# A decoder layer on one core: gram stage with broadcast decays, and 24 projection products dealt over the joins

## The chip, the cores and the metric

One core of a Trainium2 chip runs the whole program. The metric is the device time of one execution in microseconds, the median of several runs. TensorE multiplies, VectorE (DVE), ScalarE (ACT) and GpSimd (POOL) work elementwise, SyncE (SP) issues the DMAs. The matmul accumulators are eight banks of PSUM; GpSimd doesn't touch them.

## The reference, cut to what matters

The layer has three parts, each on a layernorm of x and added to x: a gated delta-rule attention with 16 heads, a cross attention, and eight experts of which one is chosen. The change touches the first alone. Inputs: 4 sequences of 512 tokens, 512 channels; a head has 128 channels for q, k, v and z.

```
qkv = silu(causal_conv4(x @ Wqkv))              # q, k, v of each head
beta = sigmoid(x @ Wb);  g = -exp(A_log) * softplus(x @ Wa + dt_bias)
q, k = l2norm(q) * DK ** -0.5, l2norm(k)
def step(M, inp):                               # M: 128 x 128 per head and sequence
    M = M * exp(g_t)
    M = M + outer(k_t, (v_t - k_t @ M) * b_t)
    o_t = q_t @ M
out = rmsnorm(o) * norm_w * silu(x @ Wz);  y = out @ Wout
```

The kernel computes the recurrence in chunks of 128 tokens. With Gamma(t) the running product of exp(g) in a chunk, it needs the decays between any two tokens of a chunk, exp(G(t) - G(s)), the decays from the chunk's beginning, exp(G(t)), the matrix of scaled products k_s . k_t under these decays, and the inverse of one plus its strict triangle.

## The kernel before

**Order.** TensorE's instructions are written out for all 16 heads. ScalarE, VectorE, GpSimd and SP have head 0, a loop over heads 1 to 14, and head 15. All queues run in program order; each wait is a semaphore wait written by hand. B = 4 sequences, NC = 4 chunks, so a [128, 512] tile usually holds one chunk of the four sequences, 128 columns each.

**Projections.** A head has 16 jobs (JOBS, line 58): K, V, Q and Z for each of the four sequences. A job is 12 products of 512 columns (4 slices of the 512 channels, each high x high, low x high and high x low of values split in two; `proj`, line 560). Seven jobs of the next head, 84 products, are done ahead (`ahead`, line 674), as a filling between dependent steps of this head: 12 before the last job, JOIN_FILL = 7, 2, 2, 1 in the joins, and FILL (60) in the chunk loop. `job_waits` (line 567) lets a job wait until its bank has been read.

**Gram stage** (the loop at line 615, per chunk c). GpSimd makes gt, the triangle times the gate's high and low parts (`decays`, line 1735). TensorE: two products of after_r with gt into bank 3 (the decays between tokens), four transposes of kT, two products of ones_r with gt (the decays from the chunk's beginning, the same in all partitions), four gram products kT x kT, and in chunks 0 and 1 six products each of the job V3. ScalarE: the exponential of the decays to pT, the squares of k with their sums (k_sq), the exponential to gam. VectorE: k_inv and cvec (reciprocal of the squared norm over beta), k_tok (a copy of the transposes), and nT = gram x pT, after GpSimd has scaled pT by cvec (`scaled`, line 1749). In chunk 3 VectorE does k_sqe and the split of the Z weights before nT.

**Jobs.** Then come Q0, Q1, Z0, Q2, Z1, Q3, Z2, 12 products ahead, Z3, with transposes of v after each Z job and of q between (`v_transpose`, `q_transpose`). The four q transposes share bank 2, and the one of sequence b waits until ScalarE has squared the one of b - 1 (qsq_done). Z0 uses the bank of V3 and waits for its convolution on VectorE.

**The inverse.** SP stores the diagonal 32x32 blocks of nT to DRAM and loads their 16x16 blocks; GpSimd inverts these by substitution (line 1783), SP stores and loads back to t32. From there TensorE joins blocks of 16 to 32, to 64, to 128 (`join16_y` to `join64_z`, lines 707 to 785), each a group of small products, with a copy on ScalarE or VectorE between two groups. GpSimd multiplies kT and qT by gam (kdT, qT), waiting for gam_done.

**Chunk loop** (line 807). The state is carried over the four chunks, with 60 products of the next head in between.

## Time and profile before

| | us |
|---|---|
| median of 3 runs | 2017.62 (2013.75 to 2017.89) |
| the profiled execution | 2019.99 |
| its span | 2018.3 |
| TensorE busy in the span | 1908.4 (95%) |
| VectorE, ScalarE, GpSimd busy | 1128.2, 933.0, 743.3 |
| mean granted clock of TensorE | 0.962 |

Times in rows are in microseconds from the span's start, of one profiled execution. PE is TensorE's matmul, PEld its weight load, DVE VectorE, ACT ScalarE, POOL GpSimd, SPq SyncE's queue. A group of instructions is told by its line and its tiles, out<-in. What stands in brackets behind a row is the idle time before it and what ended it. Busy times of consecutive matmuls overlap, since they are pipelined: their pace is that from start to start. The heads of the attention fill the span from 80 to about 1570 us; before it x is normalised and split, behind it come the output product, the cross attention and the experts.

### The profile page before, as it was taken

How to read it: one execution, taken by the hardware profiler on the slowest of the kernel's cores; microseconds unless marked ns; L12 is line 12 of the kernel's file. 1: busy time of each engine (PE TensorE's matmuls, PEld its weight loads, DVE VectorE, ACT ScalarE, POOL GpSimd, SP SyncE). 2: the span in 40 equal slices, each digit the busy share in tenths (PEclk: the TensorE clock that was granted, in tenths of full speed). 3: DMA queues.
4: the chain of work that ended last, by engine and by line, in shares of the span. 5: the costliest groups of instructions: out<-in, count | busy, mean ns of one | idle time of the engine just before them, and what ended most of it. 6: DMA issues, size and time to landing. Idle time of an engine off the chain costs nothing.

```text
span 2018.3 us, 45513 instructions
## 1 busy us (share of the span) xinstructions
PE 1908.4 (95%) x16962; PEld 1558.9 (77%) x16962; DVE 1128.2 (56%) x2048; ACT 933.0 (46%) x2987; POOL 743.3 (37%) x1143
## 2 busy tenths in 40 slices
PE   6899999999999999999999999999997799999999
PEld 4688888888888888888888788888887565656574
DVE  6656566565657465655657574656564352524333
ACT  2556464646455555646465655546463221213121
POOL 1345363645445353636264544536361000000000
PEclk9899899999989899989999998999897899999999
DMA  3011111201021111112020111111113503121200
GB/s 117 6 33 40 25 37 28 43 22 38 22 42 29 32 40 25 34 25 44 21 43 22 38 30 35 40 24 36 25 30 145 156 21 94 42 84 52 61 23 21
DMA packets 220198, 87.12 MB, mean 43 GB/s; under 512 B 138320, under 2 KB 204240, under 8 KB 219280
## 3 DMA queue, kind: packets, MB, share of 16 engines
q1 hardware_dynamic: 220048, 84.83, 16.6%
q8 instruction: 130, 2.13, 0.4%
q14 instruction: 20, 0.16, 0.0%
HBM read 57.28 MB, written 27.53 MB: 42 GB/s over the span
## 4 chain that ended last, share of the span: by engine, by line
PE 60%; issue 21%; DVE 9%; ACT 5%; POOL 4%; DMA 1%; POOLq 0%; DVEq 0%; SPq 0%; ACTq 0%
PE bank L562 27%; PE bank L871 4%; DVE vT L1383 3%; PE bank L821 3%; PE bank L830 2%; PE bank L783 2%; PE bank L772 2%; PE bank L691 2%; PE bank L815 2%; ACT vv L1084 2%; PE bank L837 1%; PE bank L934 1%; PE bank L952 1%; PE bank L669 1%; PE bank L659 1%
## 5 line engine op out<-in xcount | busy, mean ns | idle before, releaser
L562 PE MATMUL bank<-x_hi,w_hi 128*128 128x512 f32 x1024 | 429.8, 420 | 14.7 <-DVE vT L1383 14.3
L562 PE MATMUL bank<-x_hi,w_lo 128*128 128x512 f32 x1024 | 408.9, 399 | 1.8 <-issue 1.8
L562 PE MATMUL bank<-x_lo,w_hi 128*128 128x512 f32 x1024 | 406.5, 397 | 0.0
L562 PEld LDWEIGHTS bank<-x_hi,w_hi 128*128 128x128 f32 x1024 | 196.0, 191 | 55.6 <-issue 13.4
L562 PEld LDWEIGHTS bank<-x_hi,w_lo 128*128 128x128 f32 x1024 | 195.7, 191 | 45.6 <-issue 2.2
L562 PEld LDWEIGHTS bank<-x_lo,w_hi 128*128 128x128 f32 x1024 | 196.6, 192 | 32.0 <-issue 0.6
L1383 DVE SCALAR_TENSOR_TENSOR qT<-bank,cw,qT 128x511 f32<-128x511 f32 (+2 forms) x192 | 142.1, 747 | 51.0 <-ACT qT L1033 46.5
L1848 POOL TENSOR_TENSOR rstd<-ve,mhalf 128x1 f32<-128x1 f32 x32 | 17.4, 544 | 390.2 <-DVE ve L1607 390.2
L1216 ACT ACTIVATE o_tmp<-bank 128x128 f32<-128x128 f32 x256 | 67.4, 278 | 179.0 <-PE bank L837 179.0
L1383 DVE SCALAR_TENSOR_TENSOR vT<-bank,cw,vT 128x511 f32<-128x511 f32 (+2 forms) x192 | 143.0, 745 | 8.6 <-ACT vT L1033 4.1
L1383 DVE SCALAR_TENSOR_TENSOR kT<-bank,cw,kT 128x511 f32<-128x511 f32 (+2 forms) x192 | 143.4, 747 | 5.0
L1816 POOL TENSOR_TENSOR o_rstd<-o_ms,minus_half 128x4 f32<-128x4 f32 x64 | 70.5, 1101 | 200.4 <-DVE o_ms L1525 200.4
L1805 POOL TENSOR_TENSOR qT<-qT,gam 128x512 f32<-128x512 f32 x48 | 59.9, 1275 | 182.0 <-PE bank L691 182.0
L1821 POOL TENSOR_TENSOR state<-state,gam 128x512 f32<-128x512 f32 x32 | 33.6, 1051 | 209.0 <-PE bank L837 204.7
L871 PE MATMUL bank<-wo_hi,o_hi 128*128 128x512 f32 x256 | 105.4, 412 | 0.0
L871 PE MATMUL bank<-wo_hi,o_lo 128*128 128x512 f32 x256 | 100.0, 391 | 0.0
L871 PE MATMUL bank<-wo_lo,o_hi 128*128 128x512 f32 x256 | 100.0, 391 | 0.0
L1484 DVE STREAM_TRANSPOSE tT<-t 128x512 f32<-128x512 f32 x64 | 39.9, 680 | 98.3 <-DMA t<-blkT_d 98.3
L837 PE MATMUL bank<-w,pT 128*128 128x128 f32 x512 | 92.0, 277 | 0.0
L1210 ACT ACTIVATE w<-bank 128x512 f32<-128x512 f32 x64 | 38.3, 598 | 111.1 <-PE bank L821 111.1
L1118 ACT ACTIVATE nv<-bank,k_norm 128x128 f32<-128x128 f32 x256 | 72.9, 374 | 33.0 <-PE bank L669 33.0
L1788 POOL TENSOR_TENSOR prod<-blkN,blkT 128x15 f32<-128x15 f32 (+7 forms) x240 | 65.9, 275 | 54.2 <-DMA blkN<-blkN_d 36.7
(221 smaller groups left out, 4447.3 us busy)
## 6 DMA issues: line engine op xcount, KB each, us to landing
w_raw<-in_w_heads SPq DMA_DIRECT2D x64, 256.0 KB, 2.8
o_d<-og SPq DMA_DIRECT2D x64, 256.0 KB, 2.6
o_raw<-o_d SPq DMA_DIRECT2D x16, 1024.0 KB, 6.2
x_in<-in_x SPq DMA_DIRECT2D x16, 256.0 KB, 3.6
blkN_d<-nT SPq DMA_DIRECT2D x64, 64.0 KB, 2.0
t<-blkT_d SPq DMA_DIRECT2D x64, 64.0 KB, 2.4
wo_raw<-in_w_out SPq DMA_DIRECT2D x4, 1024.0 KB, 9.5
x_res<-in_x SPq DMA_DIRECT2D x16, 256.0 KB, 2.8
```

What stands on the lines that cost most here:

```text
L562: last = mm(bank[bk][:, :], w[:, kind % 2, d, :], xx[:, d, b * S:(b + 1) * S], start=(n == 0), stop=(n == 3 * ND - 1))
L691: last = mm(grid(5 + 2 * (c % 2))[:, b, :], kT[:, b, c, :], qT[:, b, c, :], start=True, stop=True)
L772: last = mm(large(half_bank(g), LATE, i, b), nT[EARLY, b, c, LATE], t32[EARLY, b, c, EARLY], start=True, stop=True)
L821: last = mm(grid(3)[:, b, :], tT[:, b, c, :], nv[:, b, c, :], start=True, stop=True)
L837: last = mm(grid(4)[:, b, :], pT[:, b, c, :], w1[:, c % 2, b, :], start=(c == 0), stop=True)
L871: last = mm(bank[c % 2][:, :], o[:, c % 2, k, :], w[:, k, :], start=(n == 0), stop=(n == 3 * H - 1))
L1118: last = fn(nv[:, b, c, :], grid(6)[:, c, :], ACT.Copy, scale=k_norm[:, b, c:c + 1])
L1216: last = fn(o_tmp[:, b, :], grid(4)[:, b, :], ACT.Square, accum_out=o_sq[:, c, b:b + 1])
L1383: stt(d[:, k:S], bank[JOB_BANK[JOBS.index((kind, b))]][:, 0:S - k], cw[:, kind, TAPS - 1 - k:TAPS - k], d[:, k:S], ALU.mult, ALU.add).then ...
L1788: tt(products, blkN[:, j, j + 1:BLK].unsqueeze(2).to_broadcast([P, below, j + 1]), blkT[:, j, 0:j + 1].unsqueeze(1).to_broadcast([P, below ...
L1805: tt(qT[:, :, c, :], qT[:, :, c, :], gam[:, :, c, :], ALU.mult).then_inc(qg_done, 1)
L1816: tt(o_rstd[:, c, :], o_ms[:, c, :], minus_half[:, 0:B], ALU.pow).then_inc(orstd_done, 1)
```

## The change

1. The decays from the chunk's beginning are no longer made by products with ones in each chunk. TensorE makes them once, for all heads, in chunk 2 of head 0 (`gam_sums`: four products with the triangle, rows are head, sequence and chunk), ScalarE takes one exponential to gam_rows, SP stores them to DRAM, and per head SP loads three chunks' rows, broadcast to all partitions (`load_gam`), behind the loads of blkN and ahead of the next K weights. gam loses chunk 0. GpSimd waits for gam_in.
2. The transposes of kT use banks 2, 0, 4, 2, and that of chunk 2 waits for nothing. The V3 job is dealt 3 products to each chunk instead of 6 and 6; its tap on ScalarE and the split of the Z weights come behind the loop.
3. VectorE makes nT of chunk c - 1 behind the key scales and k_tok of chunk c. The last nT is made from gram, cvec and pT by four steps of 128 columns, without waiting for GpSimd's scaling, which now waits for it. k_tok of chunk 3, k_sqe and the split of the Z weights come behind it.
4. The 12 products before the last job go to the joins, which now have 24: JOIN_FILL names the step ahead of which they stand.
5. In ScalarE's joins the tap of the next K1 comes behind both keep64_y. Three waits (kg, qg, sg) go from the beginning of ScalarE's head. The four semaphores at the heads' end become one.

The diff, cut to its core:

```diff
@@ -62,7 +62,8 @@
 FILL = ((0, 6), (9, 9), (9, 9), (9, 9))
-JOIN_FILL = (7, 2, 2, 1)
+JOIN_FILL = {"z16": 8, "y32_0": 4, "y32_1": 3, "z32_0": 3, "z32_1": 3, "y64_0": 1, "y64_1": 1, "z64": 1}
+assert sum(JOIN_FILL.values()) + sum(sum(f) for f in FILL) == AHEAD * 3 * ND
 HALVES = 2
...
@@ -143,7 +144,7 @@
     nT = sb("nT", [P, B, NC, P])
-    gam = sb("gam", [P, B, NC, P])
+    gam = sb("gam", [P, B, NC - 1, P])
     gt_0 = sb("gt_0", [P, 2, B, P], F32R)
...
@@ -248,13 +250,9 @@
-    def gam_bank(c):
-
-        return 4 if c else 7
-
     def ktr_bank(c):
-        return (2, 0, 0, 2)[c]
+        return (2, 0, 4, 2)[c]
...
@@ -417,6 +415,22 @@
                 sp.dma_start(o_raw[:, c % 2, :, :], o_d[:, :, b, c, :].rearrange("h p t -> p h t")).then_inc(o_in[c % 2], 16)
+
+            def load_gam(h):
+
+                if isinstance(h, int) and h == 0:
+                    sp.wait_ge(gam_done, 1)
+                    sp.dma_start(gam_d.rearrange("(i h) b c t -> (h b c) i t", i=2), gam_rows[:, :, :]).then_inc(gam_out, 16)
+                    sp.wait_ge(gam_out, 16)
+                else:
+                    sp.wait_ge(sg_done, 2 * h)
+                    hold(sp, "sp")
+                    sp.wait_ge(kg_done, 3 * h)
+                    sp.wait_ge(qg_done, 3 * h)
+                    hold(sp, "sp")
+                sp.dma_start(gam[:, :, :, :].rearrange("p b c t -> p b (c t)"),
+                             gam_d[h][:, 1:NC, :].rearrange("b c t -> b (c t)").unsqueeze(0).to_broadcast([P, B, (NC - 1) * P])
+                             ).then_inc(gam_in, 16)
...
@@ -437,6 +451,7 @@
                     sp.dma_start(blkN[rows, :, :], blkN_d[:, :, sl, sl].rearrange("k u s t -> (k u) s t")).then_inc(blkN_in, 16)
+                load_gam(h)
                 if more:
...
@@ -610,21 +624,31 @@
+            def gam_sums():
+
+                for i in range(2):
+                    for n, part in enumerate((g_hi, g_lo)):
+                        rows = part[:, i * H // 2:(i + 1) * H // 2, :, :].rearrange("p h b c -> p (h b c)").bitcast(F32)
+                        last = mm(bank[6][:, i * P:(i + 1) * P], rows, tri[:, :], start=(n == 0), stop=(n == 1))
+                last.then_inc(gam_mm, 1)
+
             def head(h, first, more):
...
                     pe.wait_ge(decay_done, 4 * h + c)
-                    hi, lo = gt[c % 2][:, 0, :, :], gt[c % 2][:, 1, :, :]
-                    mm(bank[3][:, :], after_r[:, :], hi, start=True, stop=False)
-                    mm(bank[3][:, :], after_r[:, :], lo, start=False, stop=True).then_inc(decay_mm, 1)
+                    mm(bank[3][:, :], after_r[:, :], gt[c % 2][:, 0, :, :], start=True, stop=False)
+                    mm(bank[3][:, :], after_r[:, :], gt[c % 2][:, 1, :, :], start=False, stop=True).then_inc(decay_mm, 1)
                     if c == 0:
...
                         pe.wait_ge(conv_done, 12 * h + conv_index(V_, 2) + 1)
-                    read = (0, 0, 2, 1)[c]
-                    pe.wait_ge(ksq_done, 4 * h + read)
-                    pe.wait_ge(ktok_done, 4 * h + read)
+                    if c == 2 and first:
+                        gam_sums()
+                    if c != 2:
+                        read = (0, 0, 0, 1)[c]
+                        pe.wait_ge(ksq_done, 4 * h + read)
+                        pe.wait_ge(ktok_done, 4 * h + read)
                     for b in range(B):
...
@@ -632,20 +656,13 @@
                             out_transpose(h - 1, NC - 1)
-                    pe.wait_ge(gam_done, 4 * h + c)
-                    mm(bank[gam_bank(c)][:, :], ones_r[:, :], hi, start=True, stop=False)
-                    mm(bank[gam_bank(c)][:, :], ones_r[:, :], lo, start=False, stop=True).then_inc(gam_mm, 1)
-                    if c == 1:
-                        pe.wait_ge(gam_done, 4 * h + 1)
                     pe.wait_ge(nT_done, 4 * h + max(c - 1, 0))
...
                         job_waits(h, 2 * B - 1)
-                        proj(V_, B - 1, JOB_BANK[2 * B - 1], 0, 3 * ND // 2)
-                    if c == 1:
-                        proj(V_, B - 1, JOB_BANK[2 * B - 1], 3 * ND // 2)
+                    proj(V_, B - 1, JOB_BANK[2 * B - 1], 3 * c, 3 * c + 3)
...
@@ -691,12 +710,11 @@
-                pe.wait_ge(ktok_done, 4 * h + 3)
-                pe.wait_ge(ksq_done, 4 * h + 3)
+                pe.wait_ge(ktok_done, 4 * h + 2)
+                pe.wait_ge(ksq_done, 4 * h + 2)
                 for job in range(2 * B, NJ):
                     if job == NJ - 1:
-                        ahead(3 * ND)
                         q_transpose(b - 1)
...
@@ -787,19 +806,23 @@
                 join16_y()
-                ahead(JOIN_FILL[0])
+                ahead(JOIN_FILL["z16"])
                 join16_z()
                 qk(3)
-                ahead(JOIN_FILL[1])
+                ahead(JOIN_FILL["y32_0"])
                 join32_y(0)
-                ahead(JOIN_FILL[2])
+                ahead(JOIN_FILL["y32_1"])
                 join32_y(1)
+                ahead(JOIN_FILL["z32_0"])
                 join32_z(0)
-                ahead(JOIN_FILL[3])
+                ahead(JOIN_FILL["z32_1"])
                 join32_z(1)
+                ahead(JOIN_FILL["y64_0"])
                 join64_y(0)
+                ahead(JOIN_FILL["y64_1"])
                 join64_y(1)
+                ahead(JOIN_FILL["z64"])
                 join64_z(0)
...
@@ -1083,12 +1103,11 @@
                     last.then_inc(ksq_done, 1)
-                    act.wait_ge(gam_mm, 4 * h + c + 1)
-                    fn(gam[:, :, c, :], grid(gam_bank(c)), ACT.Exp).then_inc(gam_done, 1)
-                    if c == 2:
-                        split(h, Z_)
-                    if c == 1:
-                        tap(h, V_, 3)
+                    if c == 1 and first:
+                        act.wait_ge(gam_mm, 1)
+                        fn(gam_rows[:, :, :], bank[6][:, 0:2 * P].rearrange("p (i t) -> p i t", i=2), ACT.Exp).then_inc(gam_done, 1)
+                tap(h, V_, 3)
+                split(h, Z_)
...
@@ -1195,10 +1214,10 @@
                 keep32_n(1)
+                keep64_y(0)
+                keep64_y(1)
                 if more:
                     tap(h + 1, K_, 1)
-                keep64_y(0)
-                keep64_y(1)
...
@@ -1452,13 +1470,36 @@
                     nc.vector.reciprocal(cvec[:, :, c], k_inv[:, :, c]).then_inc(cvec_done, 1)
+
+                def keys_kept(c):
                     copy(k_tok[:, :, c, :], grid(ktr_bank(c))).then_inc(ktok_done, 1)
-                    if c == 3:
-                        ts(k_sqe[:, :, :], k_sq[:, :, :], EPS_L2, None, ALU.add).then_inc(kvec_step, 1)
-                        split(h, Z_)
+
+                def masked_gram(c):
                     dve.wait_ge(gram_mm, 4 * h + c + 1)
                     tt(nT[:, :, c, :], grid(5 + 2 * (c % 2)), pT[:, :, c, :], ALU.mult).then_inc(nT_done, 1)
+
+                def last_masked_gram():
+
+                    c = NC - 1
+                    dve.wait_ge(gram_mm, 4 * h + c + 1)
+                    dve.wait_ge(cvec_done, 4 * h + c + 1)
+                    dve.wait_ge(decay_done, 4 * h + c + 1)
+                    for b in range(B):
+                        last = stt(nT[:, b, c, :], grid(5 + 2 * (c % 2))[:, b, :], cvec[:, b, c:c + 1], pT[:, b, c, :],
+                                   ALU.mult, ALU.mult)
+                    last.then_inc(nT_done, 1)
+
+                for c in range(NC):
+                    key_scales(c)
+                    if c < NC - 1:
+                        keys_kept(c)
+                    if c:
+                        masked_gram(c - 1)
+                last_masked_gram()
+                keys_kept(NC - 1)
+                ts(k_sqe[:, :, :], k_sq[:, :, :], EPS_L2, None, ALU.add).then_inc(kvec_step, 1)
+                split(h, Z_)
...
@@ -1734,7 +1772,7 @@
-                pool.wait_ge(gam_mm, 4 * h + max(c - 1, 0))
+                pool.wait_ge(decay_mm, 4 * h + max(c - 1, 0))
                 if c == 1:
...
@@ -1750,6 +1788,8 @@
                     pool.wait_ge(cvec_done, 4 * h + c + 1)
+                    if c == NC - 1:
+                        pool.wait_ge(nT_done, 4 * h + NC)
                     tt(pT[:, :, c, :], pT[:, :, c, :], spread(cvec[:, :, c]), ALU.mult).then_inc(lc_done, 1)
...
@@ -1796,13 +1836,13 @@
                                             pattern=[[0, B], [1, P]], channel_multiplier=-1).then_inc(masked, 1)
-                pool.wait_ge(gam_done, 4 * h + 4)
+                pool.wait_ge(gam_in, 16 * h + 16)
                 for c in range(1, NC):
-                    tt(kdT[:, :, c - 1, :], kT[:, :, c, :], gam[:, :, c, :], ALU.mult).then_inc(kg_done, 1)
+                    tt(kdT[:, :, c - 1, :], kT[:, :, c, :], gam[:, :, c - 1, :], ALU.mult).then_inc(kg_done, 1)
                 pool.wait_ge(qk_mm, 4 * h + 4)
                 for c in range(1, NC):
-                    tt(qT[:, :, c, :], qT[:, :, c, :], gam[:, :, c, :], ALU.mult).then_inc(qg_done, 1)
+                    tt(qT[:, :, c, :], qT[:, :, c, :], gam[:, :, c - 1, :], ALU.mult).then_inc(qg_done, 1)
```

## Rows read from the trace of the kernel before

**Rows 1.** The page, parts 1 and 2: busy times; granted clock in 40 slices.

```profile
PE 1908.4 (95%) x16962; PEld 1558.9 (77%) x16962; DVE 1128.2 (56%) x2048; ACT 933.0 (46%) x2987; POOL 743.3 (37%) x1143
...
PEclk9899899999989899989999998999897899999999
```

**Rows 2.** Windows of one head each: stretch, us, busy per engine, clock, DMA; sum last.

```profile
80.25:170.25 90.00, 87.66 (x950) 75.95 (x948) 56.64 (x95) 51.20 (x169) 43.06 (x65) 1.00 0.13 28
...
265.47:354.38 88.91, 87.66 (x956) 76.01 (x954) 56.68 (x96) 51.24 (x175) 44.92 (x68) 1.00 0.15 34
...
1099.75:1190.97 91.22, 87.85 (x955) 76.20 (x954) 56.67 (x96) 51.23 (x175) 44.85 (x68) 1.00 0.15 33
...
1378.78:1474.55 95.77, 92.42 (x956) 80.30 (x954) 56.76 (x96) 51.24 (x175) 44.98 (x68) 0.95 0.14 31
sum 1394.30, PE 1356.51 PEld 1176.67 DVE 850.97 ACT 768.48 POOL 671.20; mean PE 90.43 PEld 78.44 DVE 56.73 ACT 51.23 POOL 44.75
```

**Rows 3.** Windows inside joins: two whole joins, two late stretches, and what followed one.

```profile
309.40:323.90 14.50, 14.22 (x508) 12.18 (x509) 10.55 (x19) 8.18 (x21) 4.26 (x4) 1.00 0.01 3
...
1143.70:1160.50 16.80, 14.37 (x508) 12.36 (x509) 9.95 (x18) 8.18 (x21) 4.26 (x4) 1.00 0.02 4
...
319.90:323.90 4.00, 3.98 (x67) 3.85 (x65) 3.67 (x6) 2.25 (x4) 0.52 (x1) 1.00 0.00 0
...
222.00:225.90 3.90, 3.14 (x146) 2.30 (x139) 2.80 (x6) 2.10 (x6) 3.04 (x3) 1.00 0.02 4
225.90:232.50 6.60, 6.07 (x71) 5.91 (x70) 3.76 (x6) 2.25 (x4) 0.52 (x1) 0.64 0.00 0
```

**Rows 4.** Timeline of the gram stage: start, us, engine, line, operation, tiles; idle before.

```profile
266.91 1.28 ACT L1079 ACT_TABLE_LOAD   x1
...
268.21 0.60 ACT L1079 ACTIVATE pT<-bank 128x512 f32<-128x512 f32 x1
...
269.20 0.40 PE L619 MATMUL bank<-gt,after_r 128*128 128x512 f32 x1
...
274.16 1.05 POOL L1753 TENSOR_TENSOR pT<-pT,cvec 128x512 f32<-128x512 f32 x1
...
277.36 1.05 PE L642 MATMUL bank<-kT 128*128 128x128 f32 x8
278.17 0.47 PE L562 MATMUL bank<-x_hi,w_hi 128*128 128x512 f32 x1
```

**Rows 5.** Timeline of the gram stage's end: VectorE, and TensorE's wait.

```profile
279.41 0.73 DVE L1457 TENSOR_SCALAR k_sqe<-k_sq 128x16 f32<-128x16 f32 x1
...
280.66 0.68 DVE L1461 TENSOR_TENSOR nT<-bank,pT 128x512 f32<-128x512 f32 x1
...
281.92 2.30 DVE L1383 SCALAR_TENSOR_TENSOR vT<-bank,cw,vT 128x511 f32<-128x511 f32 x3
...
284.37 0.47 PE L562 MATMUL bank<-x_hi,w_hi 128*128 128x512 f32 x1 [0.47 <-DVE vT L1383]
```

**Rows 6.** Before the last q job: ScalarE's timeline, and the chain's moved products.

```profile
300.14 1.14 ACT L1118 ACTIVATE nv<-bank,k_norm 128x128 f32<-128x128 f32 x4
...
301.90 0.33 ACT L1100 ACTIVATE vv<-bank 128x128 f32<-128x128 f32 x1
...
300.49 2.75 PE bank L562 x12
```

**Rows 7.** Timeline where the joins begin: VectorE's and TensorE's first step.

```profile
307.17 2.49 DVE L1484 STREAM_TRANSPOSE tT<-t 128x512 f32<-128x512 f32 x4 [6.08 <-DMA t<-blkT_d]
...
309.35 1.25 PE L719 MATMUL bank<-t,nT 16*32 16x16 f32 x128 [0.24 <-ACT vv L1100]
```

**Rows 8.** DMA issue of the nearest size (KB, us to landing); kdT's writer and reader.

```profile
o_raw<-o_d SPq DMA_DIRECT2D x16, 1024.0 KB, 6.2
...
302.19 3.79 POOL L1801 TENSOR_TENSOR kdT<-kT,gam 128x512 f32<-128x512 f32 x3
...
328.11 1.16 PE L815 MATMUL bank<-state,kdT 128*128 128x128 f32 x8
```

51 lines of the change are left out of this document (23 added, 28 removed).

## The prediction

> **What bounds the kernel now.** I read the page's busy times first: TensorE is busy 95% of the span, no other engine over 56% [rows 1]. So the span is TensorE's list of work plus its waits, at whatever clock it is granted. The reader is to see next that the clock line of the same page is not all nines. I therefore cut the span into heads, from the first decay product of one head to that of the next, with the granted clock beside each [rows 2]. Fifteen such stretches take 1394.30 us. In five of them the clock was 1.00 throughout: 90.00, 88.91, 89.99, 89.32 and 91.22 us (the first, the second and the last of them are shown), together 449.44, mean 89.89. The other ten, of which the last is shown, had a part at the lower of TensorE's two levels (1.2 instead of 2.4 GHz) and take 1394.30 - 449.44 = 944.86 us, mean 94.49. A clock fall thus costs 4.6 us of a head, and the ten cost 46 us. That is the largest single sum in this profile that is neither work nor dependency.
>
> Where does it fall? The joins of a head (from the first 16x16 product to the first product with the inverse) show it. In the head that begins at 265.47 they take 14.50 us at clock 1.00; in the head before, the stretch 222.00 to 225.90 ends the full clock: there PE was busy 3.14 of 3.90 us, with 32x32 and 64x64 products only, and the stretch behind it runs at 0.64 [rows 3]. The comparable stretch of the good head had PE busy 3.98 of 4.00 us. So the clock falls where TensorE has little and small work, in the second half of the joins, where today five projection products (2, 2 and 1) stand among eight groups of small ones.
>
> **Part 1, the broadcast decays.** Each token chunk drops two products of gt with a matrix of ones. Twelve 512-column products take 2.75 us in the chain, 0.23 us each [rows 6], so eight of them are 1.8 us of TensorE work per head, and ScalarE drops four exponentials (0.6 us each, as the one in [rows 4]). Instead, four 128-column products for the whole kernel, one exponential, one store, and per head one broadcast load of 4 x 384 x 4 bytes to 128 partitions, 768 KB. Its nearest row is a 1024 KB load that lands in 6.2 us [rows 8]; by bytes that is 4.7 us, and since its pieces are others I bound it by 4 and 12 and take 6 us. It is issued behind the blkN loads, and its first reader is the kdT product at 302.19 on GpSimd [rows 8], over ten microseconds later, with the substitution between. The weight loads queued behind it on SP are read later still. Its SP waits are for events of the head before, long past. In head 0 SP waits for the store, once, some 3 us, also covered. Cost nothing; uncovered it would be up to 6 us a head.
>
> Does the removed 1.8 us shorten the gram stage? It was 12.7 us long (265.47 to 278.17) and TensorE hardly waited [rows 2, 4]. I replay it from the rows. After the first chunk's decay, transposes, gram and now three projections, TensorE is free 1 us before ScalarE has finished the table load (266.91, 1.28 us) and the exponential behind it (268.21, 0.60 us), which the next decay product waits for [rows 4]: that product starts at about 268.85 instead of 269.20. At the end GpSimd sets the pace: its fourth decay tile and the scaling of chunk 1 end at 275.2 (274.16 + 1.05 [rows 4]), VectorE then makes nT of chunk 1 (0.68 us, as in [rows 5]), and the gram product of chunk 3 waits for that: it starts at about 276.1. Before it started at 277.36 [rows 4]; the eight products less would put it at 275.6. Three projections instead of none stand behind it (+0.7). I get the end of the stage 0.5 us earlier, and two new waits of 0.3 to 0.9 us in place of the products. Bounds: 0 and -1.8 us per head.
>
> **Part 2, pipelined VectorE steps and the last product in one step.** Today k_sqe (held up to 280.14 while GpSimd works) and the weight split stand before the last nT, which ends at 281.34 [rows 5]. Behind the change the last nT needs the column vector only, not GpSimd's scaling: four 128-column steps instead of one of 512, some 1.0 us, ending near 279.1. That is 2.2 us earlier for the block inverse. But the inverse is not late now: VectorE gets t32 at 307.17, TensorE begins the joins at 309.35 when ScalarE has finished the last q squares [rows 7]. So this is slack, worth nothing by itself. k_tok of chunk 3, k_sqe and the split move behind it, in front of the convolution of V3; that convolution starts at about 281.5 against 281.92, and the Z0 job, which waited 0.47 us for it until 284.37 [rows 5], still waits, and starts 0.5 us earlier. The gain of the gram stage and this wait are the same 0.5 us.
>
> **Part 3, twelve products moved.** Twelve projections (2.75 us [rows 6]) leave the place before the last q job and go into the joins, which then hold 24. What did they cover? The next q transpose uses a bank that ScalarE still reads for the previous q squares: nv from 300.14, then squares to 302.2 [rows 6]. Without the twelve, TensorE stands from 300.5 to 302.4, so 2.0 us come back as a wait and only 0.75 us are gained. In the joins the twelve cost 2.75 us, less the waits they cover. The five full-clock heads have joins of 16.60, 14.50, 15.60, 15.00 and 16.80 us (the second and the last are shown in [rows 3]), mean 15.70, for the same list of work; so 1.2 us on average is wait beyond the clean head. There PE's busy time is 14.22 of 14.50, but the ends of small products are modelled, and each of the eight groups begins behind a copy of ScalarE or VectorE; for these handovers I estimate another 0.7 us. 2.75 - 1.2 - 0.7 = +0.8 us per head; bounds 0 and +2.75.
>
> Sum per head: -0.5 - 0.75 + 0.8 = -0.45, and -7 us over the fifteen heads that have products ahead.
>
> **Part 4, the clock.** After the change four or three products stand before each of the four 32-wide groups and one before three of the four 64-wide ones, 16 where there were 5: no stretch of the joins is left with neither large products nor full pace. I expect seven of the ten falls to go net, one or two of the remaining being new ones in the 2.0 us stand of Part 3, which has only transposes around it. 7 x 4.6 = -32 us. Bounds 0 and -46.
>
> The Trainium skill, "TensorE: Matmul & The Clock Gate", in the part on PE-mode transpose, says that transposes do not count as activity for the clock. No row here decides it. By it new falls would come at the stand of Part 3, between transposes, in as many heads as lose one in the joins; that is rival B below, at its 2011 us, and has its chance there.
>
> **Sum.** The profiled execution took 2019.99 us (span 2018.3). 2020.0 - 7 - 32 = 1981 us. The median of the runs is 2.4 us below the profiled one, so I say 1980.
>
> **Rivals.** (A) The forecast: most falls go, the schedule gains little. 1980, own range 1962 to 2000, chance 0.64.
> (B) The falls stay, at the old place or at the stand before the last q job. For it: heads with the same list of work fall and do not fall, so the granted clock hangs on something finer than the list, and the new stand after the Z2 job gives it another place. Against: the starved stretch gets eleven of the twelve products. Time 2018 - 7 = 2011, with one or two fewer 2004. Chance 0.14.
> (C) All falls go and the gram stage gives its whole 1.8 us, because GpSimd and ScalarE start their chain earlier too: per head -1.8 - 0.75 + 0.3 = -2.25, so 2018 - 34 - 46 = 1938. For it: PE at 95%. Against: the replay. Chance 0.13.
> (D) Slower. The joins are bound by TensorE itself, not by waits, so the twelve cost their full 2.75 us there, while the q bank takes 2.0 of the 2.75 us back: +2.0 us per head, +30, the gram stage gives nothing, and half of the falls stay (-23): 2025. It decides from the point where the joins grow by more than 2 us a head and fewer than six falls go. Chance 0.07.
> (E) The broadcast decays come late, so that the change does not take work off the path but puts a transfer on it: a wait on GpSimd before kdT. It would need a load over 15 us; and still TensorE first reads kdT at 328.11 [rows 8], over 20 us after GpSimd makes it. 2 in 100, with a time near 2015.
>
> **How the numbers follow.** Likeliest is A: 1980. The range that holds 8 in 10 must reach into C and B: 1952 to 2011. A measurement of this kernel can tell about 0.2%, 4 us, from no change. Faster by more: A, C and most of B, 0.87. Within: the rest of B and E, 0.07. Slower: D, 0.06.
>
> **What would show it.** Step 1: in a full-clock head the first q job starts 12.2 us after the head's first decay product instead of 12.7; ScalarE's table load ends the wait before the second decay product. Part 3: an idle time of about 2 us before a q transpose, released by ScalarE's squares. Joins: about 16 us with 24 products. Part 4: of the fifteen heads about twelve at clock 1.00, the clock line of the page nearly all nines. I am wrong if heads at clock 1.00 differ from 89.4 by more than 1.5 us, or if over six heads still show a fall.

## The result, and the profile after

The changed kernel takes 2024.44 us (median of 16 runs, 2018.74 to 2036.68), the kernel before 2017.67 (median of 16 beside it); the ratio is 1.0052, with a 95% interval of 1.0035 to 1.0070. It is slower by half a per cent, where 1980 was forecast, outside the range (1952 to 2011). Its profiled execution took 2036.68 us (span 2034.8), 16.7 more than that of before (2019.99). It is the slowest of the 16, 12.2 us above the median, with a mean granted clock of 0.973, where the median of the 16 is 0.980: what follows shows more lost clock than a usual execution of this kernel has.

The changed kernel's page: busy time and count, granted clock in 40 slices, and the broadcast load. They answer [rows 1] and the nearest load of [rows 8].

```profile
PE 1884.1 (93%) x16842; PEld 1516.1 (75%) x16842; DVE 1157.8 (57%) x2096; ACT 904.0 (44%) x2924; POOL 741.2 (36%) x1141
...
PEclk9999999999999999999799999999997899999999
...
gam<-gam_d SPq DMA_DIRECT2D x16, 768.0 KB, 4.9
```

TensorE is busy for 24.3 us less, fewer digits of the clock line lie under nine, and still the span is longer. So time went into waits. Windows of the changed kernel, one head each, columns as in [rows 2]:

```profile
453.40:545.25 91.85, 87.42 (x947) 74.57 (x946) 58.85 (x99) 49.40 (x171) 44.78 (x68) 1.00 0.17 41
...
914.03:1019.60 105.57, 99.08 (x947) 83.54 (x946) 58.38 (x99) 49.39 (x171) 44.70 (x68) 0.87 0.16 36
...
1111.60:1208.36 96.76, 89.23 (x947) 75.68 (x946) 58.81 (x99) 49.41 (x171) 44.76 (x68) 0.98 0.16 39
...
sum 1414.15, PE 1337.17 PEld 1137.60 DVE 878.98 ACT 741.37 POOL 669.62; mean PE 89.14 PEld 75.84 DVE 58.60 ACT 49.42 POOL 44.64
```

The eight heads at clock 1.00 take 92.09 us in the mean, where those of before took 89.89. Seven heads still show a fall, most of them short, one of 27 us (the second row shown). The fifteen heads are 1414.15 - 1394.30 = 19.9 us longer; the first begins 3.3 us earlier.

What TensorE waited for in heads 1 to 14 of the changed kernel (tile and line, what ended the wait; us in all, times, longest):

```profile
PE bank L676 <- ACT vv L1119: 27.6, 14, 2.0
PE bank L661 <- DVE nT L1480: 12.5, 28, 0.6
PE bank L640 <- ACT pT L1099: 10.3, 14, 0.7
PE bank L576 <- DVE vT L1401: 8.1, 14, 0.6
PE bank L749 <- issue: 5.7, 6, 2.1
...
PE bank L738 <- issue: 2.5, 1, 2.5
PE bank L710 <- issue: 2.0, 1, 2.0
```

The first row is the stand ahead of the last q job, 2.0 us in each of 14 heads. The second and third are the gram stage's new waits, 22.8 us or 1.6 us a head, against 1.8 us of products removed. The fourth is the Z0 job, which waits for VectorE's convolution of V3; the kernel before has this wait too (0.47 us, [rows 5]). The "issue" rows, waits that no semaphore ended, turned out to be the key to the rest.

The gram stage, changed kernel, head at 453.40 (answers [rows 4, 5]): VectorE, GpSimd and TensorE.

```profile
459.32 0.82 DVE L1470 SCALAR_TENSOR_TENSOR k_inv<-k_sq,beta_inv_h 128x4 f32<-128x4 f32 x1 [0.37 <-ACT vv L1104]
...
462.20 0.95 DVE L1470 SCALAR_TENSOR_TENSOR k_inv<-k_sq,beta_inv_h 128x4 f32<-128x4 f32 x1 [0.67 <-ACT vv L1104]
...
465.60 0.17 DVE L1470 SCALAR_TENSOR_TENSOR k_inv<-k_sq,beta_inv_h 128x4 f32<-128x4 f32 x1 [1.06 <-ACT vv L1104]
...
459.06 1.05 POOL L1793 TENSOR_TENSOR pT<-pT,cvec 128x512 f32<-128x512 f32 x1
...
462.08 1.05 POOL L1793 TENSOR_TENSOR pT<-pT,cvec 128x512 f32<-128x512 f32 x1
...
464.60 1.16 PE L661 MATMUL bank<-kT 128*128 128x128 f32 x8 [0.26 <-DVE nT L1480]
465.51 0.48 PE L576 MATMUL bank<-x_hi,w_hi 128*128 128x512 f32 x1
...
466.29 0.40 PE L576 MATMUL bank<-x_hi,w_hi 128*128 128x512 f32 x1
...
472.49 0.47 PE L576 MATMUL bank<-x_hi,w_hi 128*128 128x512 f32 x1 [0.57 <-DVE vT L1401]
```

An operation of four columns takes 0.17 us at 465.60, where GpSimd is idle, and 0.82 and 0.95 us where it starts under a GpSimd operation: it ends at 460.14 and 463.15, within 0.04 us of GpSimd's end (460.11, 463.13). My replay did not lengthen them. These rows alone suggest that VectorE waits for GpSimd here; no run took GpSimd's operation away. The Trainium skill ("GPSIMD Engine Reference", the specification table) has the two engines share their access to SBUF, with contention when a VectorE instruction reads two inputs from it, as this one does; the rows agree.

TensorE's rows give the end of the stage. The last gram product starts 11.2 us into the head (464.60; before 11.9, and the replay had 10.6). Three products of V3 follow (from 465.51), and the first q job starts at 466.29, 12.9 us into the head, where the kernel before starts it at 12.7 and the forecast was 12.2. So the eight products less did not shorten the stage at all.

### The profile page after: what moved, and what is told of

Its sections match the earlier page's. It is cut to its first block, busy times and chain, and to the rows that moved or that the text cites. A ratio compares the mean times of both kernels' runs of the same rounds, so it can differ in the third digit from the quotient of the medians.

```text
span 2034.8 us, 45304 instructions
## 1 busy us (share of the span) xinstructions
PE 1884.1 (93%) x16842; PEld 1516.1 (75%) x16842; DVE 1157.8 (57%) x2096; ACT 904.0 (44%) x2924; POOL 741.2 (36%) x1141
## 4 chain that ended last, share of the span: by engine, by line
PE 67%; issue 15%; ACT 9%; DVE 8%; DMA 1%; POOL 1%; ACTq 0%; DVEq 0%; SPq 0%; POOLq 0%
PE bank L576 31%; PE bank L894 4%; PE bank L844 3%; PE bank L860 3%; ACT vv L1104 3%; PE bank L838 2%; PE bank L853 2%; PE bank L859 2%; PE bank L710 2%; PE bank L791 2%; PE bank L802 2%; DVE vT L1401 2%; ACT vv L1119 2%; ACT nv L1137 2%; PE bank L957 1%
## 5 line engine op out<-in xcount | busy, mean ns | idle before, releaser
L576 PE MATMUL bank<-x_hi,w_hi 128*128 128x512 f32 x1024 | 434.6, 424 | 16.3 <-DVE vT L1401 15.8
L1793 POOL TENSOR_TENSOR pT<-pT,cvec 128x512 f32<-128x512 f32 x64 | 67.2, 1050 | 60.0 <-DVE nT L1489 51.1
L1376 DVE TENSOR_TENSOR w_lo<-w_raw,w_hi 128x512 fp32r<-128x512 f32 x64 | 47.9, 749 | 68.4 <-ACT w_hi L1045 68.4
L661 PE MATMUL bank<-kT 128*128 128x128 f32 x512 | 70.8, 281 | 14.0 <-DVE nT L1480 14.0
```

The lines of the kernel that those rows point to most:

```text
L576: last = mm(bank[bk][:, :], w[:, kind % 2, d, :], xx[:, d, b * S:(b + 1) * S], start=(n == 0), stop=(n == 3 * ND - 1))
L661: last = mm(grid(5 + 2 * (c % 2))[:, b, :], kT[:, b, c, :], kT[:, b, c, :], start=True, stop=True)
L1793: tt(pT[:, :, c, :], pT[:, :, c, :], spread(cvec[:, :, c]), ALU.mult).then_inc(lc_done, 1)
```

## The experiments

Time into the head is counted from its first decay product. "Joins begin" and "end" are the first 16x16 product and the first product with the inverse, means of the heads at clock 1.00 (e9 to e15: of all fifteen); "falls" counts the heads, of the first fifteen, in which a stretch at the lower clock begins. The first four columns are those of one profiled execution each, and that of "after" is the slowest of its kernel, so its sum stands too high against e2's. The ratio is to runs of the kernel before beside it, whose median was 2010.9 to 2017.7; it compares better than two medians of different rows. What "aligned" means stands at e9.

| kernel | joins begin, end | head | falls | 15 heads | median | ratio to before, 95% |
|---|---|---|---|---|---|---|
| before | 43.9, 59.4 | 89.9 | 10 | 1394.3 | 2017.7 | |
| after | 43.5, 61.6 | 92.1 | 7 | 1414.1 | 2024.4 | 1.0052 [1.0035, 1.0070] |
| e1 gram only | 43.9, 59.2 | 89.7 | 10 | 1393.0 | 2016.5 | 1.0021 [0.9999, 1.0043] |
| e2 products only | 43.3, 61.5 | 92.0 | 6 | 1393.6 | 2017.4 | 1.0032 [1.0007, 1.0058] |
| e3 four places | 43.5, 60.3 | 90.8 | 11 | 1392.7 | 2014.5 | 1.0006 [0.9983, 1.0030] |
| e4 three singles | 43.2, 59.8 | 90.3 | 11 | 1411.6 | 2035.5 | 1.0118 [1.0078, 1.0158] |
| e5 gated behind | 43.4, 58.7 | 89.2 | 10 | 1387.3 | 2009.2 | 0.9974 [0.9946, 1.0002] |
| e6 nine before | 43.3, 59.5 | 90.0 | 6 | 1366.4 | 1993.1 | 0.9914 [0.9880, 0.9949] |
| e7 order | 42.1, 58.5 | 89.0 | 5 | 1361.9 | 1978.9 | 0.9825 [0.9788, 0.9863] |
| e8 order, changed | 42.1, 58.7 | 89.2 | 5 | 1356.2 | 1979.5 | 0.9829 [0.9793, 0.9865] |
| e9 before, aligned | 43.8, 58.8 | 89.3 | 1 | 1339.1 | 1963.3 | 0.9756 [0.9707, 0.9805] |
| e10 before, misaligned | 43.9, 62.1 | 94.3 | 15 | 1415.0 | 2041.5 | 1.0145 [1.0094, 1.0197] |
| e11 e7, aligned | 42.0, 58.4 | 88.8 | 0 | 1332.5 | 1953.9 | 0.9717 [0.9668, 0.9766] |
| e12 e8, store behind | 41.5, 59.5 | 90.0 | 4 | 1349.3 | 1972.9 | 0.9804 [0.9755, 0.9853] |
| e13 after, aligned | 43.5, 61.6 | 92.1 | 1 | 1381.6 | 2006.8 | 0.9974 [0.9953, 0.9995] |
| e14 e12, aligned | 41.6, 57.8 | 88.2 | 0 | 1323.6 | 1947.5 | 0.9676 [0.9643, 0.9708] |
| e15 e1, aligned | 44.0, 58.8 | 89.2 | 0 | 1338.3 | 1965.1 | 0.9763 [0.9730, 0.9796] |

### The change in two halves

**e1** is the changed kernel with the old dealing of the products, so the gram parts alone; **e2** the kernel before with the new dealing alone.

```diff
 e1 (on after)
-JOIN_FILL = {"z16": 8, "y32_0": 4, "y32_1": 3, "z32_0": 3, "z32_1": 3, "y64_0": 1, "y64_1": 1, "z64": 1}
+JOIN_FILL = {"z16": 7, "y32_0": 2, "y32_1": 2, "z32_0": 0, "z32_1": 1, "y64_0": 0, "y64_1": 0, "z64": 0}
                     if job == NJ - 1:
+                        ahead(12)
                         q_transpose(b - 1)
```

> The changed kernel with the twelve products put back before the last job (JOIN_FILL 7, 2, 2, 1 as before): the gram stage and the broadcast decays alone. Theory P (the fillings are what costs): a full-clock head falls from 92.1 to 90.1 us, joins from 18.1 to about 15.6 us, some ten of fifteen heads lose clock as before, time within 0.3% of before. Rival G (the gram stage is what costs, by the convolution of V3 coming later): full-clock heads stay above 91.5 us and the time stays near 2024.

> The kernel before with only the twelve products moved into the joins (8, 4, 3, 3, 3, 1, 1, 1) and the tap of K1 behind keep64_y. Theory P: full-clock head 89.9 + 2.6 (joins) - 0.7 (before the last job) = 91.8 us, heads with a clock fall from ten to about five, time about 2022 to 2028. Rival G: full-clock head 90.5 or less and a time under 2000, since the falls go and nothing else is paid.

The gram parts neither lengthen nor shorten a head by more than 0.2 us; the dealing gives the whole of the longer head (92.0) and, in e2, the whole of the falls' change. The ratios of the two, 1.0021 and 1.0032, make the 1.0052 of the whole change. So the joins hold the question.

### Where a product in the joins costs

**e3** deals the changed kernel's 24 products over four places instead of eight; **e4** keeps the kernel before and moves three of the twelve into the three 64-wide places, one each.

```diff
 e3 (on after)
+JOIN_FILL = {"z16": 10, "y32_0": 5, "y32_1": 5, "z32_0": 0, "z32_1": 4, "y64_0": 0, "y64_1": 0, "z64": 0}
 e4 (on before)
+JOIN_FILL = {"z16": 7, "y32_0": 2, "y32_1": 2, "z32_0": 0, "z32_1": 1, "y64_0": 1, "y64_1": 1, "z64": 1}
-                        ahead(3 * ND)
+                        ahead(9)
```

> The changed kernel with the same 24 products in the joins at four places (10, 5, 5, 0, 4, 0, 0, 0) instead of eight. Theory S (each switch from small products to a large one and back costs 0.25 us beside the product): joins of full-clock heads 18.1 - 4 x 0.27 = 17.0 us, the step between the two first 64-wide groups back from 1.5 to 1.0 us, head 91.0. Rival W (only the work counts, or the places cover waits): joins stay at 18.1 us or grow. On the clock: with no large products in the 64-wide part the falls come back to ten of fifteen if it is that part that drops the clock.

> The kernel before with three of the twelve products moved to single places before the second-half groups (one each before y64_0, y64_1 and z64; nine stay before the last job). Theory S: each single costs 0.5 us, so full-clock joins grow by 1.5 us to about 17.2 us, the place before the last job gives 0.7 back, head 90.7; falls drop below ten of fifteen if these places are what keeps the clock. Rival W: each costs 0.23 us, joins 16.4 us, head 89.9.

The same 24 products cost 1.3 us a head less at four places than at eight (joins 16.8 instead of 18.1), about 0.3 us for each place given up. Three single products made the undisturbed joins 1.4 us longer (16.0 in e4's cleanest head, 14.6 before), nearly 0.5 each, where a product in a row costs 0.23. The heads at clock 1.00 are only 0.4 us longer than before; the rest of e4's 1.2% lies in longer falls (four heads at a mean clock of 0.91 to 0.93, before one), for which no run gives the reason. The rows show the price of a single product. First the kernel before, where the two 64-wide y groups run as one, then e4 with a product between them (TensorE's timeline; start, us):

```profile
319.87 2.07 PE L772 MATMUL bank<-t,nT 64*64 64x64 f32 x32
```

```profile
322.27 1.14 PE L773 MATMUL bank<-t,nT 64*64 64x64 f32 x16
323.35 0.51 PE L563 MATMUL bank<-x_lo,w_hi 128*128 128x512 f32 x1
323.78 1.14 PE L773 MATMUL bank<-t,nT 64*64 64x64 f32 x16
```

From the first half to the second it is 1.51 us, where a group of 32 takes 2.07 in all. No semaphore is waited for. The groups had run back to back before: there was nothing for a product to cover, and the change from small to full products and back costs about 0.27 us beside the product's own 0.23.

### The gram stage's lost half microsecond

The Z0 job starts 19.1 us into the head instead of 18.9, and the transposes of v behind it at 21.9 instead of 21.7. VectorE's convolution of V3, for which Z0 waits, starts at 16.6 (470.04; before 16.45) where I had worked out 16.0. **e5** is e1 with that convolution ahead of the gated output of the head before.

```diff
+                conv(h, V_, 3)
                 if not first:
                     gated(h - 1, NC - 1)
-                conv(h, V_, 3)
```

> As e1_gram_only, and VectorE does the convolution of V3 before the gated product of the head before, not behind it (0.66 us of work moved off its way). Theory V (the 0.6 us that the gram stage gives TensorE is lost again at the Z0 job, which waits for that convolution): the first v transpose comes at 21.3 us of the head instead of 21.9, the wait of 0.57 us goes, full-clock heads 0.5 us shorter than in e1_gram_only (about 89.2). Rival: the Z0 job has another late input (split weights, bank), and the v transpose stays at 21.9.

The transposes of v then start at 21.25, Z0's wait is gone, and the heads are about 0.5 us shorter. I had read this as the forecast's 0.5 us, held back by the convolution, and the expectations of e5, e8 and e15 say so ("0.6 us"). That reading was wrong: the first products behind the stage, at 12.1, are the last three of V3, and the q job starts at 12.9 in e1 and e5 too. What e5 gains is the wait for the convolution, which the kernel before has as well: without its 0.47 us the transposes there would start at 21.7 - 0.5 = 21.2, as in e5. That is an estimate; no run moved the convolution on the kernel before.

### What the place ahead of the last job is worth

**e6** (kernel before) leaves nine products there and deals 15 over four join places. **e7** (kernel before) runs the last job ahead of the last two q transposes, four products between them, and 20 at four places; ScalarE's squares are then covered by a job that has to be done anyway. **e8** is the same on the changed kernel with the edit of e5.

```diff
 e7
-                    if job == NJ - 1:
-                        ahead(3 * ND)
-                        q_transpose(b - 1)
                     whole_job(h, job)
+                    if job == NJ - 1:
+                        q_transpose(b - 1)
                     if kind == Z_:
                         v_transpose(b)
+                        if job == NJ - 1:
+                            ahead(4)
```

> The kernel before with nine products ahead of the last job and fifteen in the joins at the old four places (6, 3, 3, 0, 3). Theory N (nine of the twelve had been free there, hidden behind ScalarE's squares): second last q transpose at 37.0 instead of 37.6, three products more in the joins cost 0.7, full-clock head 89.9, as before. On the clock: if it is large products among the 32-wide groups that keep it, falls go from ten of fifteen to about six; if products at the 64-wide groups are needed, they stay at ten.

> The kernel before with the last job (Z3) ahead of the q transpose that waits for ScalarE's squares, then v transpose, four products, q transpose; joins 8, 4, 4, 0, 4 at the old four places. The last job covers the wait, so products can go to the joins without a stand. Theory: full-clock head 89.5 to 90.5, no stand before the transpose, clock falls in at most three of fifteen heads, time 1970 to 1985. Rival F (falls hang on the 64-wide groups alone): falls stay at about ten, time 2005 or more.

> The same order and fillings on the changed kernel, with the gated product behind the convolution of V3 as in e5_gated_behind. Theory: as e7_order with the gram stage 0.6 us shorter: full-clock head about 89.2, time 5 to 10 us under e7_order. Rival: the broadcast decays and the pipelined VectorE steps give nothing even so, time equal to e7_order within 0.2%.

With nine products the q transpose comes at the same time as with none: nine of the twelve were free where they stood. e7 gains another 0.9 us a head, and with the falls it is 1.75% faster than the kernel before. e8 was no faster, although its last nT is ready 1.7 us earlier in the head: its joins begin at 41.6 to 43.6 us, now here, now there, and three of its five falls follow such a late beginning. SyncE's waits and TensorE's first join product, e8, head at 441.85:

```profile
SPq L324 <- DVE og L1462: 2.7, 1, 2.7
```

```profile
485.20 1.25 PE L740 MATMUL bank<-t,nT 16*32 16x16 f32 x128 [1.79 <-DMA t<-blkT_d]
```

SyncE stands at the wait for the gated tile, which e5's edit had put later, with the loads of blkN behind it, and with them the whole inverse. **e12** moves that store behind the loads:

```diff
-                if not first:
-                    sp.wait_ge(og_done, 4 * h)
-                    hold(sp, "sp")
-                    store_gated(h - 1, NC - 1)
                 sp.wait_ge(blkN_out, 64 * h + 64)
                 ...
+                if not first:
+                    ...
+                    store_gated(h - 1, NC - 1)
                 load_gam(h)
```

> The changed kernel with the changed order, and in SyncE's queue the store of the last gated tile of the head before (which waits for VectorE) behind the loads of blkN instead of ahead of them. In the trace SyncE stood up to 2.7 us at that wait with the loads behind it, and the first product of the joins then waited up to 1.8 us for the blocks' load. If that wait is what made the start of the joins vary from 41.6 to 43.6 us into the head: joins begin at 41.6 to 41.8 in all heads, 0.6 us a head, the whole 1965 to 1972 instead of 1979.5, since heads with an idle time at an instruction load stay. If ScalarE's last squares set it anyway: 1978 to 1980.

The joins begin at 41.5 in every head but the first (41.3), where e7's begin at 42.0, and the kernel takes 6.7 us less, at the edge of what was expected (1972.9; 1965 to 1972). The inverted blocks land at 39.6 in the mean and nothing waits for them; in e7 they land at 41.5 in the mean, which would be too late in some heads. So the slack that I had called worth nothing is needed here, together with the convolution of e5; no run takes the two apart.

### Why some heads fall and others don't

In [rows 2, 3] heads with one list of work did and did not show a fall, and I left that as "something finer than the list". The trace has it. The kernel before, head at 170.25: TensorE's timeline, two of the transfers' rows for 223.5 to 225.5 us, and four windows (columns as in [rows 2]).

```profile
222.26 0.50 PE L562 MATMUL bank<-x_hi,w_hi 128*128 128x512 f32 x1
222.60 0.40 PE L562 MATMUL bank<-x_lo,w_hi 128*128 128x512 f32 x1
...
224.00 0.50 PE L562 MATMUL bank<-x_hi,w_lo 128*128 128x512 f32 x1
...
226.43 0.22 PE L758 MATMUL bank<-tT,y 32*32 32x32 f32 x2 [1.22 <-issue]
```

```profile
DMA packets 1, 0.02 MB, mean 8 GB/s; under 512 B 0, under 2 KB 0, under 8 KB 0
...
q8 instruction: 1, 0.02, 3.5%
```

```profile
223.80:225.20 1.40, 1.33 (x67) 0.90 (x59) 1.03 (x3) 0.99 (x3) 1.24 (x2) 1.00 0.05 12
225.20:226.40 1.20, 0.01 (x2) 0.00 (x0) 0.00 (x0) 0.00 (x0) 0.00 (x0) 1.00 0.00 0
226.40:227.70 1.30, 1.27 (x24) 1.23 (x24) 0.92 (x3) 0.94 (x2) 0.00 (x0) 1.00 0.00 0
227.70:237.90 10.20, 10.20 (x69) 9.50 (x68) 4.21 (x7) 1.90 (x4) 0.52 (x1) 0.50 0.09 28
```

For 1.2 us all engines stand, no semaphore is missing, and the only transfer about is one of the instruction queue: 16 KB, from 223.94 to 225.08. Such a stand of TensorE that no semaphore ends I call a hole. Within 1.3 us of the hole's end the clock is at its lower level. I then numbered TensorE's instructions, a weight load and a matmul as one each and each separate wait as one. Every hole of over 0.55 us in the joins of the first fifteen heads of e7 and e8 stands at number 193 or 194 modulo 256, and ends 1.2 to 1.6 us after such a load has landed; the same numbers come out of the traces of all the other runs. In the kernel before, too, all ten heads that fall have a hole of 0.6 to 2.3 us at that number, which begins ahead of the fall; of the other five, two have one (1.3 and 1.8 us, at the 128-wide qk products) and don't fall. A head has 1954 instructions there (1936 in the changed kernel), seven times 256 and a rest, so that the place wanders from head to head. Among 512-column products, 0.12 us an instruction, the load is in long before; 256 instructions of the 16-wide products are gone in 1.25 us, less than a load (0.9 to 1.9 us, in the median 1.0) and the 1.2 to 1.6 behind it.

The Trainium skill ("Runtime: NRT & Kernel Launch", Instruction fetch mechanics) tells of blocks of 16 KiB or 256 instructions; the size of the loads and the distance of the holes agree. It also says that the loading stays hidden; in these joins it doesn't, and here the measurement decides.

**e9, e10 and e11** put spare instructions (waits on a semaphore that was set at the start) among the products of the eight jobs ahead of the joins, so that a head has 2048 and the place stands still (two such waits of the code are one instruction of the trace: e9's page has 46994 instructions, that of before 45513, which is 71 + 15 x 94 more): in e9 where the kernel before had a head without a hole, in e10 where it had 1.0 to 1.4 us of one, in e11 on top of e7.

```diff
+SPARE = (71, 94)          # e9; e10: (212, 94), e11: (188, 94); head 0, other heads
...
+            def spare(n):
+                if n:
+                    for _ in range(2 * n):
+                        pe.wait_ge(masks_set, 1)
...
+                    if n:
+                        spare(extra * n // (3 * ND - 1) - extra * (n - 1) // (3 * ND - 1))
                     last = mm(bank[bk][:, :], w[:, kind % 2, d, :], xx[:, d, b * S:(b + 1) * S],
```

> The kernel before, with nothing changed but 94 spare TensorE instructions per head (waits on a semaphore that is long set; 71 in head 0), dealt over the eight whole jobs ahead of the joins. Of the traces so far, every idle time of TensorE in the joins that no semaphore ended stands at instruction 193 or 194 modulo 256 of TensorE's stream, and ends 1.2 to 1.5 us after a 16 KB load of the instruction queue has landed. A head has 1954 instructions, so that this place wanders through the joins from head to head; with 94 more it is 2048, eight times 256, and each head has it where the third head of the kernel before has it (the one from 265.47 us, 88.91 us long, no fall). Theory F, falls come from instruction loading: no fall in heads 1 to 14, each 88.9 us and up to 1.5 us for the spare instructions, the fifteen heads 1334 to 1357 us instead of 1394, the whole 1958 to 1980. Theory C, falls hang on the density of the work alone and the place is chance: 9 to 10 heads fall as before, the whole 2018 or, with the spare instructions, up to 2035.

> The same kernel with the same 94 spare instructions per head, but 212 instead of 71 in head 0, so that the place is the same in all heads again, now where the heads with 1.0 to 1.4 us of idle time among the 32-wide products had it (95.1 and 95.8 us long, each with a fall). Theory F: an idle time near 1 us among the 32-wide products and a fall behind it in all of heads 1 to 14, each 95 to 96 us, the whole 2045 to 2060. Theory C: the same time as with 71, within 5 us.

> The kernel with the changed order (last product job ahead of the last transposes, 8, 4, 4, 0 and 4 products in the joins), with 94 spare instructions per head and 188 in head 0: the place stands where its heads of 88.6 to 88.9 us had it. Theory F: all heads 88.6 to 89.5 us and no fall, the fifteen heads 1332 to 1343 us instead of 1361.9, the whole 1950 to 1960 instead of 1979. Theory C: five or six falls stay, 1979.

TensorE's longest "issue" waits in heads 1 to 14, first of the kernel before, then of e9, then of e10 (their lines 738, 766 and 768 are 730, 758 and 760 of the kernel before), and the last window row of e10:

```profile
PE bank L730 <- issue: 7.5, 13, 2.3
...
PE bank L758 <- issue: 5.2, 5, 1.4
...
PE bank L760 <- issue: 2.3, 2, 1.3
```

```profile
PE bank L738 <- issue: 7.7, 14, 2.9
```

```profile
PE bank L768 <- issue: 14.0, 14, 1.2
```

```profile
1401.94:1495.33 93.39, 91.14 (x955) 79.16 (x954) 56.76 (x96) 51.15 (x175) 44.88 (x68) 0.96 0.14 32
```

The two kernels differ in 141 idle instructions in head 0 and in nothing else, and are 78 us apart. e10 has its hole among the 32-wide products in all 14 heads, and a fall in each; e9 has no hole there and one fall, in the one head whose 16-wide hole is 2.9 us long. e9 is 2.4% faster than the kernel before with the same work. e10's heads were 1 us shorter than expected (93 to 95.3), its whole 3.5 us below the range, its direction and place as expected. The spare instructions cost nothing that can be read: six of e9's heads take 88.87 to 88.91, as the shortest of before (88.91).

**e13 and e15** align the changed kernel and the gram parts (112 spare instructions; 169 and 73 in head 0), **e14** aligns e12 (112 and 220). Each puts the place where good heads had it, which need not be the same step of the joins in each kernel.

> The changed kernel with 112 spare instructions per head (169 in head 0), so that all its heads are 2048 instructions apart and have the places of instruction loading where its heads of 91.9 to 92.4 us had them. The kernel before so aligned took 1963.3, its fifteen heads 1339.1. Theory T (the change itself costs TensorE time in the joins, and what it wins back is only falls that instruction loading had made): no fall in the joins, heads 92.0 to 92.4, at most a few short falls at the stand ahead of the last job, the fifteen heads 1380 to 1390 instead of 1414, the whole 1988 to 2000, 1.3 to 1.9% slower than the kernel before in the same alignment. Against it: if the joins' 24 products were only in the way of instruction loading, the changed kernel would come down to 1963, too.

> The changed kernel with the old dealing of products (12 ahead of the last job, 12 in the joins), that is the gram parts alone, in the alignment of the aligned kernel before. What the gram stage is worth when no fall hides it: it began its first job 0.6 us earlier, and its Z0 job not earlier. Theory T: heads 89.0 to 89.3, the whole within 4 us of 1963. If the eight products less are worth their 1.8 us a head: 1936.

> The kernel with the changed order and SyncE's store behind the loads, with 112 spare instructions per head (220 in head 0), so that all heads have the places of instruction loading where its heads of 87.9 us had them: heads 87.9 to 88.4, no fall in fourteen of them, the fifteen heads 1320 to 1328 instead of 1349.3, the whole 1943 to 1950.

The sums of the fifteen heads' windows, of e9 and e13, then e13's longest wait of TensorE, and the sum of e14:

```profile
sum 1339.13, PE 1316.34 PEld 1141.44 DVE 850.17 ACT 767.35 POOL 669.66; mean PE 87.76 PEld 76.10 DVE 56.68 ACT 51.16 POOL 44.64
```

```profile
sum 1381.61, PE 1315.03 PEld 1121.21 DVE 874.80 ACT 741.30 POOL 672.32; mean PE 87.67 PEld 74.75 DVE 58.32 ACT 49.42 POOL 44.82
```

```profile
PE bank L684 <- ACT vv L1127: 27.6, 14, 2.0
```

```profile
sum 1323.55, PE 1297.32 PEld 1116.34 DVE 874.99 ACT 739.62 POOL 672.48; mean PE 86.49 PEld 74.42 DVE 58.33 ACT 49.31 POOL 44.83
```

With the places still, the change costs 1381.6 - 1339.1 = 42.5 us, 2.8 us a head, and 2.2% of the whole (2006.8 against 1963.3). e13's heads came as expected, its whole 7 us above, because I had taken off the median what was worked out for the profiled execution. All of it lies in the joins (18.1 instead of 15.0 us); they begin 0.3 us earlier. Instruction loading and its falls cost the kernel before 1394.3 - 1339.1 = 55.2 us in its profiled execution, the changed one 1414.1 - 1381.6 = 32.5 in its slowest. The ratios in the table, over all runs, give 2.4% or 49 us for the kernel before (1 and 0.9756) and 0.8% or 16 us for the changed one (1.0052 and 0.9974): 33 us less. The gram parts alone (e15) change nothing that can be measured (1965.1 against 1963.3); together with the order, the convolution and the store moved, they bring e14 to 1947.5, 0.3% below e11 and 3.2% below the kernel before.

## Why the prediction was wrong

The schedule was forecast to give 7 us and cost 42.5 in the same 15 heads once the places stand still; the clock was forecast to give 32 and gave about that over all runs. So the miss of 44 us is the schedule's, and in it the joins': 2018 + 42.5 - 33 = 2027, against 2024 measured. Both signs of being wrong that the prediction named came: heads at clock 1.00 take 92.09 us, 2.7 off its 89.4, and seven heads fall.

The profiled execution alone would tell it otherwise. It is 55.7 us above the sum of 1981: the heads at full clock are 92.09 instead of 89.44 (15 x 2.65 = 40 us), the falls gave back 13 us instead of 32 (1394.3 - 15 x 89.89 = 46 before, 1414.1 - 15 x 92.09 = 33 after), and the first head began 3.3 us earlier.

- **Joins, +0.8: the step that failed.** They grew by 2.6 us over the mean of before, and by 3.1 with the places still (15.0 to 18.1). From clean joins to clean joins it is 3.5 us (14.55 in e9 to 18.05 in e13): the twelve products cost their full 2.75, as rival D had it, and four more places, at about 0.27 us each, account for the rest (3.8 in all, a little too much). Of what I took off, the 0.7 for handovers was nothing, since the groups ran back to back (I had the row, 14.22 busy of 14.50, and argued it away with "the ends are modelled"). The 1.2 us beyond the clean head were waits, but for instructions: they stand where the 256th instruction falls, not where I put the products.
- **The clock, -32: right in size over the runs, with a wrong reading under it.** The 13 us above are those of the slowest execution. In e2, which has the same products in the joins and whose profiled execution lies at its median, the falls cost 1393.6 - 15 x 92.0 = 14 us, 32 less than before; the ratios say 33, the holes' own time included. What I read from [rows 3] was wrong: the stretch 222.00 to 225.90 holds no 64-wide group, but 32-wide ones and three full-size products (222.26, 222.60, 224.00), and its missing busy time is the hole from 225.2 on. It wasn't the small work that let the clock fall there, but the hole in it; e9 keeps the clock in all heads but one with the same twelve products. With more products among them no hole is left in the 32-wide steps (the waits of after have no "issue" row between lines 763 and 779), and the long falls went, but for one of 27 us. Holes of 2.0 to 2.5 us stayed in the 16-wide steps and at qk in four heads, each with a fall. New falls came at the stand, in three heads of after and in eleven of e3, each 3.4 us long and costing 1.6 us. They lie between transposes, as rival B had it, and cost a third of what it set. The Trainium skill ("TensorE: Matmul & The Clock Gate", PE-mode transpose) says that a transpose doesn't count as a busy TensorE in the same way. These falls don't contradict it, but they don't show it either: the stand is in all fifteen heads and only three fall, and holes of this length among 16-wide products, with no transpose near, are followed by falls as well.
- **Gram stage, -0.5: wrong too, it gave nothing.** The first q job starts at 12.9 where 12.2 was forecast and the kernel before has 12.7, and Z0 starts 0.2 us later instead of 0.5 earlier. The new waits are three (0.73, 0.65 and 0.26 us) where I had two; with 1.6 us they take back nearly all of the 1.8. VectorE's short operations under GpSimd's, 1.4 us in two chunks, were not in the replay, and the last gram product, which waits for VectorE's nT, starts 0.6 us later than in it.
- **Part 3, -0.75 with a stand of 2.0: right.** 1.97 us in each head; joins begin 0.6 us earlier in e2, 0.4 in after. What I missed is that most of these products were free where they stood, so that any price in the joins was too much.
- **The broadcast load: right.** It lands in 4.9 us, covered, and nothing waits for it. The earlier nT (1.7 us, 2.2 forecast) was slack, as said, up to the order of e12, whose joins begin before the blocks of e7 would have landed in some heads.
- **Chances.** Rival D was the case that came, in its mechanism (the twelve at full price, a gram stage that gives nothing, a stand of 2.0 us) and nearly in its time (2025), and had 0.07. It had no price for the four places and set 23 us for the falls that go, about 10 too few; that the two nearly cancel is luck. I had made the sum from [rows 3] with the one reading under which products in the joins are nearly free.

## What to carry over

Ask of a filler whether the place it goes to has a wait at all, and of the place it leaves whether it was free there; between groups of small products that run back to back it costs its own time and a change of form. In a long stream of small TensorE instructions, look for waits that end with "issue", number the instructions and see whether they stand at one place modulo 256: then a few idle instructions elsewhere can be worth more than the schedule, and two versions with different instruction counts can't be compared without aligning them. Look where the profiled execution lies among the runs before its sums are set against the forecast. To find where a job starts, count the products: the first ones behind a stage may belong to the job before. A step moved on VectorE holds every queue that waits for it in order, SyncE's too.

## What the runs showed of the hardware that I had not expected

- TensorE's instructions come in loads of 16 KB, and the holes stand 256 instructions apart. Where small products use them up faster, it stands until 1.2 to 1.6 us after the load has landed, for 2.9 us at the most (e9). Such a hole of 1 us among 32-wide products was followed by a clock fall in every head of e10.
- A fall of 10.2 us costs about 5 us, one of 3.4 us some 1.6. The kernel before varied by 20 us from run to run (2004 to 2024 beside e9), e9 by 6, e14 by 3, in four runs each. The slower executions of one kernel are those with the lower mean granted clock (after: 2018.7 us at 0.982, 2036.7 at 0.973), so most of the scatter came from falls.
- One full-size product between two groups of 64-wide ones costs 0.50 us instead of 0.23.
- A VectorE operation of four columns with two inputs in SBUF took 0.17 us alone and up to 0.95 us where it started under a GpSimd operation.
